# Two bf16 bit patterns per edge in the sort of a graph kernel, one of them partly made on ScalarE

## The reference

```python
edge_index = jnp.stack([src, dst])
...
row, col = (edge_index[0], edge_index[1])
edge_feature = jax.nn.silu(edge_rbf @ We1 + be1) @ We2 + be2
msg = edge_feature * x[col]
agg = jax.ops.segment_sum(msg, row, num_segments=N_NODES)
return x + (jax.nn.silu(agg @ Wn1 + bn1) @ Wn2 + bn2)
```

## Time and profile before

| | us |
|---|---|
| median of 3 runs | 1191.53 (1191.32 to 1192.52) |
| profiled execution | 1190.32 |
| its span | 1188.5 |
| PE busy | 1153.4 (97%) |
| DVE busy | 850.0 (72%) |
| ACT busy | 680.2 (57%) |
| POOL busy | 422.8 (36%) |

### The profile page before, as it was taken

The page is one execution under the profiler, slowest core; times in us unless marked ns, Lnnn a source line. Parts: engine busy times, 40 slices in busy tenths (PEclk is TensorE's granted clock), DMA queues, the critical chain, the costliest instruction groups (busy, mean ns, idle before and its releaser), DMA issues.

```text
span 1188.5 us, 20926 instructions
## 1 busy us (share of the span) xinstructions
PE 1153.4 (97%) x6268; PEld 969.4 (82%) x6268; DVE 850.0 (72%) x1479; ACT 680.2 (57%) x1351; POOL 422.8 (36%) x546
## 2 busy tenths in 40 slices
PE   6999899999999999999999999998899999999997
PEld 3678788888888888888888888886789888798786
DVE  8888677777777777777777777777977234175664
ACT  3576676676767667676766767674634223142352
POOL 2003465656656555555655555541500000001000
PEclk9999999999999999999999999998899999999999
DMA  8623522222222222222222222220101102022101
GB/s 262 265 101 138 209 84 71 86 71 86 77 76 88 69 86 70 87 75 79 82 73 86 68 87 71 84 76 27 45 1 45 63 21 85 0 72 71 45 1 45
DMA packets 26965, 95.86 MB, mean 81 GB/s; under 512 B 6533, under 2 KB 6783, under 8 KB 22578
## 3 DMA queue, kind: packets, MB, share of 16 engines
q0 software_dynamic: 18592, 54.42, 15.3%
q1 hardware_dynamic: 8208, 40.84, 9.7%
q10 hardware_dynamic: 130, 0.13, 0.0%
HBM read 86.52 MB, written 8.85 MB: 80 GB/s over the span
## 4 chain that ended last, share of the span: by engine, by line
PE 91%; DVE 5%; ACT 2%; issue 1%; DMA 0%; DVEq 0%
PE ps L1004 13%; PE ps L1006 12%; PE ps L1005 12%; PE ps L997 9%; PE ps L998 9%; PE ps L999 9%; PE ps L1050 4%; PE ps L1012 3%; PE ps L1011 3%; PE ps L1111 3%; PE ps L1110 3%; PE ps L1038 2%; PE ps L1115 2%; PE ps L1035 1%; PE ps L1247 1%
## 5 line engine op out<-in xcount | busy, mean ns | idle before, releaser
L1004 PE MATMUL ps<-we_hi,s_hi 128*128 128x512 f32 x664 | 267.2, 402 | 0.0
L1005 PE MATMUL ps<-we_lo,s_hi 128*128 128x512 f32 x664 | 259.8, 391 | 0.0
L1006 PE MATMUL ps<-we_hi,s_lo 128*128 128x512 f32 x664 | 259.7, 391 | 0.0
L577 POOL DMA_INDIRECT xg<-h_dram,node_picks x166 | 176.9, 1065 | 96.6 <-POOL node_picks L567 66.1
L718 ACT ACTIVATE m_hi<-msg 128x512 fp32r<-128x512 f32 x166 | 105.0, 632 | 158.0 <-DVE msg L1669 158.0
L571 POOL DMA_INDIRECT rbf<-in_edge,edge_picks x166 | 171.6, 1034 | 50.5 <-issue 32.0
L1674 DVE TENSOR_TENSOR m_lo<-msg,m_hi 128x512 fp32r<-128x512 f32 x166 | 114.9, 692 | 59.3 <-ACT m_hi L718 59.3
L1662 DVE TENSOR_TENSOR s_lo<-s,s_hi 128x1024 fp32r<-128x1024 f32 x83 | 101.7, 1226 | 76.5 <-ACT s_hi L712 76.5
L1006 PEld LDWEIGHTS ps<-we_hi,s_lo 128*128 128x128 f32 x664 | 124.7, 188 | 27.4
L1004 PEld LDWEIGHTS ps<-we_hi,s_hi 128*128 128x128 f32 x664 | 125.2, 189 | 21.1
L1005 PEld LDWEIGHTS ps<-we_lo,s_hi 128*128 128x128 f32 x664 | 125.4, 189 | 20.6
(11 more groups left out here) (301 smaller groups left out, 2556.2 us busy)
## 6 DMA issues: line engine op xcount, KB each, us to landing
fold_dram<-folded SPq DMA_DIRECT2D x6, 1024.0 KB, 4.7
wstage<-fold_dram SPq DMA_DIRECT2D x6, 1024.0 KB, 4.8
plain<-in_fold_a SPq DMA_DIRECT2D x3, 1024.0 KB, 9.5
plain<-in_fold_b SPq DMA_DIRECT2D x3, 1024.0 KB, 11.5
stage<-in_fold_a SPq DMA_DIRECT2D x3, 1024.0 KB, 17.0
stage<-in_fold_b SPq DMA_DIRECT2D x3, 1024.0 KB, 24.3
w_raw<-in_nodew SPq DMA_DIRECT2D x3, 1024.0 KB, 10.7
wstage<-in_selfw SPq DMA_DIRECT2D x3, 1024.0 KB, 5.1
```

The source lines that it names most:

```text
L577: pool.indirect_dma_start(xg[t.slot][:, j], None, h_dram, bass.IndirectOffsetOnAxis(ap=node_picks[t.slot][:, j:j + 1], axis=0)).then_inc(x ...
L1004: pe.matmul(outp, lh, rh, start=False, stop=False, skip_group_check=True)
L1005: pe.matmul(outp, lh, rl, start=False, stop=False, skip_group_check=True)
L1006: return pe.matmul(outp, ll, rh, start=False, stop=False, skip_group_check=True)
```

## The change

Each edge now has two 32-bit words whose upper halves are bf16 bit patterns. The first holds the edge's number plus 128 and the parity of the destination as sign; the second holds the quarter of (destination plus 128) as exponent, the next bit of it as sign and the source modulo 128 as mantissa. Both are placed with one-hots as before, so a column has two matmuls in place of three, both into bank 0. VectorE makes the words with integer operations: six ahead of the wait for the rank products, five behind `hi16`. The one-hots and products become bf16 (the iotas and positions stay f16). VectorE makes both products of an even group and the first of an odd one; ScalarE makes the second of an odd group, with six instructions, one for each column, of 128 elements at a step of two. `slot_tables` takes the words apart with shifts and masks, eleven operations; GpSimd's wait is now met by `slot_edge` and `slot_dst`, of which the latter comes last.

```diff
-KEY_ONE, KEY_SHIFT, KEY_P = 127 << 10, 13, 7
-DUOS = GROUP // 2
+HALF_WORD = 16
+EDGE_FROM, DST_FROM = 128, 128
+EDGE_BITS = (1 << 15) - 1
+ACT_EVERY = 2
...
-        hot_lo = [hot_at(f"hot_lo{i}", [EP, GROUP // 2, P, 2], F16) for i in range(HOT_RING)]
-        hot_hi = [hot_at(f"hot_hi{i}", [EP, GROUP // 2, TILES, 2], F16) for i in range(HOT_RING)]
+        hot_lo = [hot_at(f"hot_lo{i}", [EP, GROUP // 2, P, 2], BF16) for i in range(HOT_RING)]
+        hot_hi = [hot_at(f"hot_hi{i}", [EP, GROUP // 2, TILES, 2], BF16) for i in range(HOT_RING)]
...
             def mark(i):
 
-                act.wait_ge(keys_ready, 1)
+                if i % ACT_EVERY == 0:
+                    return
+                act.wait_ge(ends_typed, 4)
                 act.wait_ge(hots_lo_made, i + 1)
-                for j in range(DUOS):
-                    n = i * DUOS + j
-                    act.activation(keyed[i % HOT_RING][:, j], hot_lo[i % HOT_RING][:, j], ACT.Copy,
-                                   scale=keys[:, n:n + 1].bitcast(F32)).then_inc(marks_made, 1)
+                for j in range(GROUP):
+                    n = i * GROUP + j
+                    act.activation(ended[i % HOT_RING][:, 1, j // 2, :, j % 2], hot_lo[i % HOT_RING][:, j // 2, :, j % 2],
+                                   ACT.Copy, scale=second_half[:, n:n + 1].bitcast(F32)).then_inc(marks_made, 1)
...
                 pe.wait_ge(hots_hi_made, i + 1)
-                pe.wait_ge(marks_made, (i + 1) * DUOS)
+                pe.wait_ge(marks_made, (i + 1) // ACT_EVERY * GROUP)
                 pe.wait_ge(ends_made, i + 1)
                 r = i % HOT_RING
                 for j in range(min(GROUP, ET - i * GROUP)):
-                    at = j % 2 * REGION
                     slots = hot_hi[r][:, j // 2, :, j % 2]
-                    pe.matmul(ps[:, 5, at:at + TILES], keyed[r][:, j // 2, :, j % 2], slots,
-                              start=False, stop=False, skip_group_check=True)
                     for v in range(2):
...
-            dve.memset(ps[:, 5], 0.0).then_inc(perm_zeroed, 1)
             dve.memset(ps[:, 0, 0:2 * REGION - 32], 0.0).then_inc(perm_zeroed, 1)
             dve.memset(ends16[:], 0.0).then_inc(ends_typed, 1)
+            dve.memset(second_half[:], 0).then_inc(ends_typed, 1)
...
+            dve.tensor_scalar(dst_up[:], dst_i[:], float(DST_FROM), None, ALU.add).then_inc(halves_made, 1)
+            dve.tensor_scalar(edge_half[:], edge_no[:], HALF_WORD, None, ALU.logical_shift_left).then_inc(halves_made, 1)
...
-            dve.wait_ge(ends_typed, 1)
-            dve.tensor_scalar(ends16[:, 1, 0:ET], src_f[:], 1.0, None, ALU.add).then_inc(ends_typed, 1)
-            dve.wait_ge(dst_in, 16)
-            dve.tensor_copy(ends16[:, 0, 0:ET], dst_i[:]).then_inc(ends_typed, 1)
-            dve.wait_ge(consts_ready, 8)
-            dve.tensor_scalar(keys[:], key_no[:], KEY_SHIFT, None, ALU.logical_shift_left).then_inc(keys_ready, 1)
+            dve.wait_ge(halves_made, 6)
+            dve.tensor_tensor(first_half[:], odd_bit[:], edge_half[:, 0:ET], op=ALU.bitwise_or).then_inc(halves_made, 1)
+            dve.tensor_tensor(low_bits[:], src_bits[:], dst_bits[:], op=ALU.bitwise_or).then_inc(halves_made, 1)
+            dve.wait_ge(ends_typed, 2)
+            dve.wait_ge(halves_made, 7)
+            dve.tensor_copy(ends16[:, 0, 0:ET], first_half[:].bitcast(F32)).then_inc(ends_typed, 1)
+            dve.wait_ge(halves_made, 8)
+            dve.tensor_tensor(second_half[:, 0:ET], low_bits[:], half_bit[:], op=ALU.bitwise_or).then_inc(ends_typed, 1)
+            dve.wait_ge(ends_typed, 4)
+            dve.tensor_copy(ends16[:, 1, 0:ET], second_half[:, 0:ET].bitcast(F32)).then_inc(ends_typed, 1)
...
                 dve.wait_ge(hots_lo_made, i + 1)
-                for v in range(2):
+                for v in range(1 if i % ACT_EVERY else 2):
                     mm = dve.tensor_tensor(ended[r][:, v], hot_lo[r][:],
```

## The result

The changed kernel takes 1185.8 us (median of 5 runs, 1185.44 to 1187.42), the kernel before beside it 1191.53 (5 runs, 1190.52 to 1192.95): ratio 0.995, 95% interval 0.9939 to 0.9961. It is faster by 0.5%, 5.7 us, just under half of the 11.66 forecast, and outside the range of 1177.5 to 1184 on the slow side. The profiled execution took 1185.44 us, 4.88 less than the one before (span 1183.7 against 1188.5).

A forecast was written before the change was run, and what follows sets the result against it. TensorE was taken to set the pace. Removing 165 matmuls saves 12.44 us, less 0.78 for a later first group, so 11.66: 1178.7 us for the profiled execution, 1179.9 for the median, range 1177.5 to 1184.

The forecast's parts named there:

- The sum of the sort: TensorE in the edge sort: 165 fewer matmuls at 75.4 ns save 12.44 us, less 0.78, leaving 11.66.
- The five operations: VectorE behind hi16: five operations in place of three start the first hot_lo 0.78 us later, paid in full by TensorE.
- because group 0 is already late: TensorE's first place: it comes straight behind ended, so VectorE's 0.78 us delay was counted in full.
- The six: VectorE between counts and the rank-product wait: six integer operations take 0.93 us, covered with 0.2 to spare.
- ScalarE's narrow products: ScalarE in odd groups of the sort: six half-width products at 0.30 us each, 1.8 us per odd group.
- the rival in which they cost as much as wide ones: ScalarE's narrow products take 0.406 us each, making TensorE wait 2.2 us in all, 1182.1; chance 0.12.
- The slower rival: VectorE compares f16 tiles into bf16 at half rate, group 27 is 4.9 us later, 1196.4; chance 0.06.
- The three tight places: First fold units, units (2,1) to (3,0), units (3,0) to (4,0): VectorE and ScalarE keep up; TensorE's beat falls to 4.6 us.
- The last factors' late load: Rival: the load issued after the fourth fold_lo lands at 95.3, wanted at 92.5, costing 2.8 us, 1182.7; chance 0.04.
- The wait for rT_lo: Tail behind the sort: TensorE's wait before the first rT_lo stays as long as now.
- everything behind, the edge loop included, moves forward as a block: After 122 us: all later work, edge loop included, keeps the whole 11.66 us gain.
- the gain is given back in the tail by a wait: Rival: a wait the rows don't show in the tail behind the sort leaves the time within 0.2%; chance 0.04.

The follow-up runs named there:

- e1: Changed kernel with the dropped tile half_i put back, unused, so the edge loop's tiles lie 672 bytes higher, where they lay before; 1179.63 us, ratio 0.9888.
- e3: Changed kernel with 160 unused bytes in front of the edge loop's tiles; 1178.83 us, ratio 0.9886.
- e10: Kernel before with 448 unused bytes in front of the loop's tiles, bringing them to 96 modulo 512; 1188.47 us, ratio 0.9967.
- e9: Changed kernel with 96 unused bytes in front of the loop's tiles, timed again; 1175.44 us, ratio 0.9861.
- e2: Kernel before with half_i moved to another region, so the loop's tiles lie 672 bytes lower, as in the changed kernel; 1199.65 us, ratio 1.0061.
- e7: Changed kernel with 416 unused bytes in front of the loop's tiles, a we2 to s distance of 256 modulo 512; 1180.63 us.
- e14: e9 with the weights we1 moved from 160 to 96 modulo 512, the same place as rT; 1183.5 us.
- e15: Changed kernel with the loop's tiles at 0, we1 at 64 and we2 at 0 modulo 512; 1176.91 us, ratio 0.9883.
- e13: e9 with the weights we2 moved from 160 to 0 modulo 512; 1182.1 us.
- e6: Changed kernel with we2 moved from 160 to 0 modulo 512, the loop's tiles keeping their place modulo 512; 1177.36 us (one run).

## Why the prediction was half right

**The sum of the sort: right in size.** The 165 products at 75.4 ns were all on the path. With the tiles of before, the change brings 1192.48 to 1179.63 (e1) and 1178.83 (e3), with those of e10 and e9 13.0 us; the forecast was 11.66, and 1179.9 for the median. In the profiled pair 11.43 us had been gained when the loop began. The 1.2 and 2.0 us more of e1 and e3 lie within their intervals (0.9867 to 0.9909 is 5 us wide); for e9 against e10 there is no interval. In the profiled pair the sum is 12.44 - 0.89 for the late first place - 0.09 for the wait before rT_lo, 11.46.

**The five operations: undersized by 0.3, and what TensorE pays for them was misread.** 0.78 was forecast, 1.10 measured at hot_lo: the casts from the bit patterns take 0.37 us, not the 0.24 that I took from the other casts of this size, and the next instruction starts 0.29 and 0.47 after them, where I had 0.15 and 0.27. TensorE's first place is 0.89 later (23.13 - 22.24). The prediction lets TensorE pay in full "because group 0 is already late", but the row at 22.24 has no idle time before it: TensorE came straight from its fold unit, and ended had been ready for 0.27 us. Here are the row before it and the first place of e1, which has no idle time either (the changed kernel's has 0.28, above):

```profile
17.52 4.88 PE L1050 MATMUL ps<-plain 128*128 128x512 f32 x11
```

```profile
23.56 1.07 PE L1041 MATMUL ps<-hot_hi,ended 125*128 125x166 bf16 x12
```

The first place comes when both the fold unit and ended are through. The fold unit's end is another one in each execution: its matmuls follow each other after 0.85 us at first and after 0.43 from about 13.4 us on in the profile of before, 14.3 in that of after and 16.0 in that of e1. So of the 0.89, 0.45 is the fold unit's own later end (its last matmul starts at 22.26 against 21.81) and 0.44 is the wait for VectorE (0.28 of it counted as idle, from the modelled end of that matmul). In e1 the five operations cost TensorE nothing, in e9 its idle time before the first place is 0.78. That the term came out near 0.89 is luck in part.

**The six: right.** Their cover held, total_i at 10.54 as before.

**ScalarE's narrow products: right.** 1.91 us for six in an odd group, forecast 1.8 to 1.9. That fells the rival in which they cost as much as wide ones (2.44). One has 427 ns in it and the six 1.91 us, so they follow each other after (1.91 - 0.427) / 5 = 0.297. The Trainium skill's formula (VectorE: DVE Perf Modes, The TRN2 errata — SBUF-src ops pay a fixed extra latency per instruction; the prediction names another section of that page) gives 0.293, and the trace agrees.

**The slower rival fell.** The comparison of f16 tiles into bf16 has 551 ns in the groups above; before, with f16 throughout, it had 548:

```profile
L1563 DVE TENSOR_TENSOR hot_lo<-iota_lo,lo 125x768 f16<-125x768 f16 x28 | 15.3, 548 | 4.5 <-PE ps L1038 4.5
```

The Trainium skill (Vector Engine (DVE) Microarchitecture Reference, 5.1) asks for two-byte types and not for equal ones; here it is shown with two sources.

**The three tight places: right.** No gap before a place in units (3,0) to (4,0), 4.60 us a beat; of all places only the first waited, the 0.28 us of its row above in 0.3 for all:

```profile
L1040 PE MATMUL ps<-hot_hi,ended 125*128 125x166 bf16 x330 | 27.4, 237 | 0.3 <-DVE ended L1587 0.3
```

The last factors' late load did not come about either: fold_hi started at 99.43. The wait for rT_lo grew from 1.09 to 1.18, which is all that the tail gave back.

**The step that failed** is the one sentence in the sum: "everything behind, the edge loop included, moves forward as a block". The loop moved forward by 11.43 us and then ran 0.08 us a step slower over 83 steps (8.433 against 8.351), 0.082 x 83 = 6.8 us. 11.43 - 6.8 = 4.6, against 4.8 in the span. The loop has no term in the sum, and the prediction gives no reason for that; the diff changes none of its instructions. I gave the rival "the gain is given back in the tail by a wait" 0.04. What was given back was no wait, and it wasn't in the tail: it was the pace of 24 of the step's matmuls. The tiles' lower place is its cause, since e1 brings the pace back with one unused tile and e2 takes it from the kernel before. The whole diff did show it, as a removed line that allocates half_i. The loop's share was the one to look at first, since it is 56% of the span: one per cent of its pace is 6.7 us, more than half of what the edit was worth.

## What to carry to other kernels

An edit that adds, drops or resizes a tile moves every tile allocated behind it, and that can change the pace of a matmul stream that it doesn't touch. Before the gain of such an edit is judged, put the later tiles back to their old addresses with an unused tile (one line) and time that too; here the verdict on the same edit is 0.5% or 1.1% by that line. Where one matmul loop fills the time, a few pads in the placement are cheap experiments of their own: e9 is the changed kernel and 96 unused bytes, 0.9% faster. And compare an unedited loop in the two traces by a record that comes once a step, at its beginning and at its end, before looking for waits.

## What the runs showed of the hardware

- The pace of the f32 matmuls of 512 and 256 columns depends on where their two SBUF operands lie, mostly on how they lie to each other; a distance of 0 and one of 256 bytes have the same times (e1 and e7). e14 and e15 show that the distance isn't all. With no gap on TensorE and a granted clock of 1.00, a block of 12 took 2.83 or 2.89 us, a first layer 1.48 or 1.54, a whole step 8.29 to 8.43. Rounding to 32 bytes alone doesn't protect from it: all tiles here have that.
- No collision with another engine's accesses to s or to we2 is needed for it: moving we2, which only TensorE reads in the loop (the column tables behind it moved along), switched it on (e13) and off (e6).
- A cast that reads 165 words as f32 and writes bf16 took 370 ns on VectorE, one from int32 to f16 of the same size 240.
- ScalarE reading and writing two-byte elements at a step of two, 128 of them, followed each other after 0.297 us, where 256 without a step took 0.406. The rows' 0.104 less for half the width would give 0.302, so the step has no price that shows.
- At the kernel's start TensorE's f32 matmuls of 512 columns followed each other after 0.85 us and then after 0.43; the change came at 13.3 us in the profile of e9, at 17.5 in that of e7. e1 and e3, with their tiles at the same place modulo 512, have it at 16.0 and 13.9. The first place was at 23.14 us in e9 and at 24.81 in e7.
